# Ordering two engines in a channel-mix loop: one drain added on VectorE, one removed on ScalarE

## The reference

```python
# attention part
scores = einsum(q, k) / sqrt(1024)
sign_mask = sign(scores); sign_mask += (sign_mask == 0)
masked = where(causal, scores * sign_mask, -inf)     # = |scores| below the diagonal
out = softmax(masked) @ v;   x = x + (out @ Wo.T + bo)
# channel mix
y      = layernorm(x)
y_prev = y shifted by one token (zeros in front)
xr = mu_r * y + (1 - mu_r) * y_prev
xk = mu_k * y + (1 - mu_k) * y_prev
r  = sigmoid(xr @ W_r.T)
k  = square(relu(xk @ W_k.T))
x  = x + r * (k @ W_v.T)
```

## Time and profile before

| | |
|---|---|
| timed runs | 5030.85 and 5294.17 us, median 5162.51 us |
| profiled execution, its own time | 5030.06 us |
| its span (slowest of 8 cores) | 5027.9 us |
| spans of the 8 cores | 5013.8 to 5027.9 us |
| mean granted TensorE clock | 0.938 to 0.940 on all cores |
| TensorE busy over the span | 4155.9 us (83%) |
| VectorE, ScalarE, GpSimd busy | 32%, 9%, 19% |

### The profile page before, as it was taken

One profiled execution on the slowest core, in us unless ns is written; L12 is line 12 of the kernel. 1 busy time (PEld: TensorE's weight loads), 2 busy tenths in 40 slices (PEclk: granted clock), 3 DMA queues, 4 the chain that ended last, 5 costly groups with the idle time before them and its releaser, 6 DMA issues.

```text
span 5027.9 us, 64517 instructions; the slowest of 8 cores (5013.8 to 5027.9 us)
## 1 busy us (share of the span) xinstructions
PE 4155.9 (83%) x24576; PEld 2384.0 (47%) x24576; DVE 1595.1 (32%) x3657; ACT 466.5 (9%) x1048; POOL 931.2 (19%) x908
## 2 busy tenths in 40 slices
PE   1999999999568986899877999987667888888888
PEld 0444444444234433444433444443346777777777
DVE  2233333322231233123232232323344434434342
ACT  2000000000010111011100011110011111111111
POOL 4222222222211101111002101100332112121211
PEclk7999999999779997999988999998879999999999
DMA  5111111111444114311116121112331101101010
GB/s 156 51 59 59 63 61 60 45 43 50 134 102 66 34 34 109 59 34 34 49 53 122 13 64 38 34 40 61 71 89 42 51 26 51 43 34 51 26 43 18
DMA packets 185423, 285.91 MB, mean 57 GB/s; under 512 B 19360, under 2 KB 124064, under 8 KB 184608
## 3 DMA queue, kind: packets, MB, share of 16 engines
q1 hardware_dynamic: 99232, 193.69, 13.1%
q10 hardware_dynamic: 50688, 67.13, 3.7%
q0 software_dynamic: 35200, 20.98, 3.5%
HBM read 197.84 MB, written 100.66 MB: 59 GB/s over the span
## 4 chain that ended last, share of the span: by engine, by line
PE 73%; DVE 12%; issue 4%; POOL 4%; DMA 2%; ACT 2%; DVEq 2%; SPq 1%; ACTq 0%; POOLq 0%
PE ps_b L108 12%; PE ps_a L108 12%; PE ps_d L108 11%; PE ps_d L134 11%; PE ps_c L134 11%; PE ps_c L108 10%; DVEq L99 2%; DVE o_sb L1081 1%; DVE ploT L1047 1%; POOL plo L1022 1%; DVE of L801 1%; PE ps_c L120 1%; DVE at_bk L1193 1%; ACT p_sb L1012 1%; POOL yT_lo L376 1%
## 5 line engine op out<-in xcount | busy, mean ns | idle before, releaser
L1022 POOL TENSOR_TENSOR plo<-p_sb,phi 128x512 bf16<-128x512 f32 (+3 forms) x144 | 154.4, 1072 | 1586.7 <-DVE phi L1016 1586.7
L134 PE MATMUL ps_d<-vhiT,phiT 128*128 128x512 bf16 x544 | 222.6, 409 | 49.4 <-DVE ploT L1047 49.4
L451 POOL TENSOR_TENSOR qk_l<-qk_f,qk_h 128x512 bf16<-128x512 f32 x128 | 147.7, 1154 | 561.5 <-DVE qk_h L445 561.5
L134 PE MATMUL ps_c<-vhiT,phiT 128*128 128x512 bf16 x512 | 202.6, 396 | 48.8 <-DVE ploT L1047 48.8
L108 PE MATMUL ps_a<-khiT,qhiT 128*128 128x512 bf16 (+2 forms) x576 | 203.3, 357 | 46.3 <-DMA qloT<-sql 46.3
L692 POOL TENSOR_TENSOR xr_lo<-xrf,xr_hi 128x256 bf16<-128x256 f32 x128 | 86.2, 674 | 820.0 <-DVE xk_hi L686 811.3
L134 PE MATMUL ps_d<-vloT,phiT 128*128 128x512 bf16 x544 | 222.8, 410 | 0.0
L134 PE MATMUL ps_d<-vhiT,ploT 128*128 128x512 bf16 x544 | 221.5, 407 | 0.0
L108 PE MATMUL ps_a<-yT_hi,wq_hi 128*128 128x512 bf16 x256 | 105.6, 413 | 139.8 <-POOL yT_lo L376 60.2
L108 PE MATMUL ps_b<-khiT,qhiT 128*128 128x512 bf16 (+1 forms) x576 | 212.2, 368 | 0.0
L108 PE MATMUL ps_b<-kloT,qhiT 128*128 128x512 bf16 (+1 forms) x576 | 212.2, 368 | 0.0
(11 more groups left out here) (248 smaller groups left out, 9723.6 us busy)
## 6 DMA issues: line engine op xcount, KB each, us to landing
khiT<-skh SPq DMA_DIRECT2D x152, 128.0 KB, 4.2
kloT<-skl SPq DMA_DIRECT2D x152, 128.0 KB, 4.2
vhiT<-svh SPq DMA_DIRECT2D x76, 256.0 KB, 5.5
vloT<-svl SPq DMA_DIRECT2D x76, 256.0 KB, 5.7
sx<-x SPq DMA_DIRECT2D x32, 512.0 KB, 15.4
sx<-at_bk POOLq DMA_DIRECT2D x64, 256.0 KB, 4.6
xin<-sx SPq DMA_DIRECT2D x32, 512.0 KB, 4.2
x1c<-sx SPq DMA_DIRECT2D x32, 512.0 KB, 4.8
```

What stands on the lines that cost most here:

```text
L134: e.matmul(o, ww, mm, start=s, stop=sp),
L451: e.tensor_tensor(d, s, h, op=OP.subtract), inc="gv")
L1022: e.tensor_tensor(d, s_, h, op=OP.subtract), inc="gv")
```

## The change

On VectorE a drain is recorded between the copy of the last column into `sliv` (L662) and the difference `d1c` (L665) in every chunk: 8 chunks in 16 units, 128 drains. On ScalarE the drain in front of the Relu (L757) is left out, once for each of the 8 products in 16 units, 128 drains. The waits, the operations, their operands and their order stay as they were. The instruction in front of the removed drain's waits is another drain, behind the previous Square (L765), or a Sigmoid at the start of stage two.

```diff
@@ -660,6 +660,7 @@
             p.drain("vector")
             p.op("vector", lambda e, d=sliv.ap()[:, c:c + 1],
                  s=yc.ap()[:, 256:257]: e.tensor_copy(d, s))
+            p.drain("vector")
             p.op("vector", lambda e, d=d1c[par].ap(), a=yc.ap()[:, 1:257],
                  b_=yc.ap()[:, 0:256]:
                  e.tensor_tensor(d, a, b_, op=OP.subtract))
@@ -754,7 +755,6 @@
                 tok_mm = p.mm_group(psH[parh][:, 0:256], mms)
             p.wait("scalar", tok_mm)
             p.waits("scalar", [th2[mp], tl2[mp]])
-            p.drain("scalar")
             psH_free[parh] = p.op("scalar", lambda e, d=e_sb[mp].ap(),
                                   s=psH[parh][:, 0:256]:
                                   e.activation(d, s, AF.Relu), inc="sv")
```

## The result

The changed kernel is slower by 0.24%: ratio of its runs to those of the kernel before 1.0024, 95% interval 1.0017 to 1.0032. On 5030 us the ratio comes to 12.1 us, from 8.6 to 16.1; the prediction's sum had 10.8, or 0.21%. The profiled execution took 5045.42 us.

What follows compares the result with a forecast made beforehand. The prediction took TensorE's waits for GpSimd and VectorE, behind chunks 4 to 7, to bound the channel mix. It summed 5030.1 + 11.6 (VectorE drains) - 0.8 (ScalarE drain) to 5041 us, range on record 5019 to 5180.

Steps and rivals of the forecast that it cites:

- The path: Channel mix: chunks 4 to 7 of each unit lie on the path with their VectorE time, chunks 0 to 3 don't.
- The price of the VectorE drain: Between L662 and L665: 0.17 us per drain, 68 drains on the path, 11.6 us in all.
- The first rival: Added VectorE drain is free, only ScalarE's gain is left: 5029.3 us; chance 13%.
- The price of the ScalarE drain: In front of the Relu: removing it gains 0.05 us once per unit, 15 times, 0.8 us in all.
- "No slack at chunks 5 and 6": At L801 behind chunks 5 and 6: the chain enters from VectorE, so nothing absorbs the 0.17 us drain.
- The clock: TensorE clock falls behind the k_lo wait, 1.67 us each, in 5 of 14 even units: change priced at nothing.
- the 3 to 8: Test for the clock: wrong if the count of 4.30 us products in stage three leaves this range.
- the second rival: A clock fall in every unit behind the longer k_lo wait: 16.7 us more, 5057.6 us; chance 17%.
- the third rival: Each of four growing waits per unit brings a clock fall, 55 more, 92 us, 5133 us; chance 4%.
- The sum: Whole kernel: 5030.1 + 11.6 - 0.8 = 5040.9, so 5041 us, 0.2% more; chance 65%.
- The threshold: About 2% (100 us) can be told from no change, so 0.2% more would count as the same.

Runs made afterwards that it cites:

- e3: Kernel before plus the VectorE drain in chunks 0 to 3 only: unit 79.04 us, phase three -1.2 us, ratio 0.999.
- e4: Kernel before plus the VectorE drain in chunk 4 only: unit 79.21 us, phase three +3.1 us (4 cores).
- e5: Kernel before plus the VectorE drain in chunks 5 and 6 only: unit 79.19 us, phase three +3.9 us, ratio 1.0005.
- e6: Kernel before plus the VectorE drain in chunk 7 only: unit 79.21 us, phase three +2.9 us.
- e8: Changed kernel (both edits) with all chunks placed early, in stages one and two: unit 73.63 us, phase three -89.9 us, ratio 0.9877 against the kernel before.
- e2: Kernel before with only the ScalarE drain in front of the Relu left out: unit 79.00 us, phase three -2.3 us, ratio 0.999.
- e1: Kernel before with only the VectorE drain added, the ScalarE drain kept: unit 79.52 us, phase three +14.5 us (6 cores), ratio 1.0028.
- e9: Kernel before with chunk 7 alone made 0.40 us longer by drains and a repeated copy: unit 79.45 us, phase three +10.3 us.
- e10: Kernel before with chunk 4 alone made 0.40 us longer by drains and a repeated copy: unit 79.45 us, phase three +10.8 us.
- e13: Kernel before with the transposes of chunks 0 and 1 made twice, 0.44 us more TensorE work: unit 79.48 us, phase three +11.6 us.
- e11: Kernel before with chunk 7 made 0.88 us longer by drains and three more copies: unit 79.90 us, phase three +23.6 us.

## Why the prediction was right or wrong

**The path, right.** That VectorE, 41% busy, is on the path at four of eight chunks, and that chunks 0 to 3 are hidden: e3 to e6 show it chunk by chunk, e8 from the other side.

**The price of the VectorE drain, right.** 0.17 us predicted by the start-to-start step of the reciprocal, 0.16 measured. The first rival, that the drain is free, is out. The prediction set beside it the Trainium skill, "VectorE: DVE Perf Modes", section "The DRAIN you can't avoid", and took from it only the sentence that the next operation waits for the pipe to empty. The same section says that a next operation that isn't held starts earlier, and the trace is of that kind: `d1c` started 0.07 us after the start of a copy of 0.15 us, and only the explicit drain moved it to 0.23.

**The price of the ScalarE drain, right.** 0.05 us predicted from what a passed wait costs, 0.05 measured in the trace, and 0.05 a unit in e2 (0.03 from e1 to the changed kernel).

**"No slack at chunks 5 and 6", wrong.** The step that failed is "the chain enters L801 from VectorE and not from the matmuls, so there is no slack". The chain names what ended last by its records, and two releasers 0.1 us apart look like one. The start of L801 against the cast in front of it, 0.29 us instead of the 0.21 between the two casts, was there to be read. It put 2 x 14 x 0.09 = 2.5 us too many into the sum.

**The clock, wrong.** The step that failed is "I price this at nothing in the sum". The falls rose by 3.25 to 8.75, outside the 3 to 8 that the prediction had set as its own test, and that is 5.4 us or 40% of the loss. The row was read rightly: each fall is 1.67 us, at just that place. What failed was to leave the average outcome out because no single outcome was sure; halfway to the second rival's ten more would have been 8 us. And the reason given for the rival, "behind the longer wait", was wrong too: between 79.05 and 79.5 us the count follows the unit's length, whatever makes it longer (e9, e10, e13). Nor did the third rival's falls behind all four waits come; only at 0.88 us more did a second place start (e11).

**The sum.** 11.6 - 0.8 = 10.8 became 13.4 in phase three of the profiled run: 8.6 for the drains with the ScalarE gain in it, and 5.4 for the falls, less 0.6. Two errors of opposite sign brought the total nearer than its parts, and that is luck. The threshold was badly chosen as well: I wrote that 2% is about what can be told from no change and called the outcome the same. The interval of the ratio is 0.15% wide, and a loss of 0.24% is clear of zero. The sign was in the sum and should have been the forecast. The level of 5041 us stands 0.4% under the median after, 5062.6 us, which the stated range holds.

## What to carry to other kernels

A drain costs only what is behind it on the path, so find out where the instruction stands before its price; here the 56 drains in chunks 0 to 3 of the even units cost nothing (e3), and moving all of the chunks to a covered place won seven times what the edit lost. Where two engines reach a meeting point within 0.1 us of each other, the chain names one of them and hides the other's slack: compare the step with the same step elsewhere. And where a loop has falls of the clock in some turns, a change of the turn's length, even by useful work, can change how many; price the average and not the certain part.

## What the runs showed of the hardware

An explicit drain on VectorE behind a 128x1 copy delays the next operation by 0.16 us (0.23 against 0.07 from start to start), and on ScalarE with nothing in flight a drain costs 0.05 us (0.25 against 0.20 behind the product). The number of clock falls in a steady loop moved from 4.9 and 5.5 to 8.9 of 14 when a unit grew by 0.44 us, with the waits unchanged (e13): I had expected it to depend on how long TensorE waits. That it does so as well beyond some length is shown only by e11, at 2.3 us.
